# A macaron block with mixture-of-experts layers: indirect transfers of two kinds without an upper bound for their indices

## The reference

```python
x = x + 0.5 * ffn(layernorm(x))      # mixture of experts
x = x + attn(layernorm(x))           # gate, long convolution, gated projections
x = x + 0.5 * ffn(layernorm(x))      # the same mixture again

def ffn(x):                          # E = 12 experts, K = 3 for each token, hidden size 512
    gate_logits = x @ Wg
    topw, sel = top_k(gate_logits, 3); topw = softmax(topw)
    h = gelu(x @ Wup[e] + bup[e])    # for each expert e that the token chose
    y = h @ Wdown[e] + bdown[e]
    return sum over the 3 experts of topw * y
```

## Time and profile before

| | |
|---|---|
| median of 3 runs | 943.9 us (943.35 to 944.24) |
| span of the profiled execution, first to last instruction | 623.9 us |
| outside the span | 320.0 us by the median |
| PE busy | 560.0 us |
| ACT busy | 514.5 us |
| GpSimd (POOL) busy | 416.4 us |
| DVE busy | 373.2 us |

### The profile page before, as it was taken

How to read it: one execution, slowest core, us unless ns; L and a number is a source line. 1 busy time by engine, 2 the same in 40 slices (tenths; PEclk the granted TensorE clock), 3 DMA queues, 4 the chain that set the end, 5 groups by cost and what they waited for, 6 DMA issues and landing times.

```text
span 623.9 us, 17393 instructions
## 1 busy us (share of the span) xinstructions
PE 560.0 (90%) x4527; PEld 522.7 (84%) x4527; DVE 373.2 (60%) x1735; ACT 514.5 (82%) x1462; POOL 416.4 (67%) x424
## 2 busy tenths in 40 slices
PE   7559879999999999999899799998798799999995
PEld 6449779999999888878889688787698799999992
DVE  7947788653111577888865679987828532232224
ACT  3557777599998989899889699998589679998984
POOL 1074557677776777327677777777777777777770
PEclk9999988899999999999999799999799989999997
DMA  7996242343454343312255333332264532433264
GB/s 192 323 222 190 63 113 67 86 123 87 128 161 128 104 119 101 80 45 67 72 169 133 90 87 98 90 98 70 69 153 109 131 87 70 117 87 83 61 225 136
DMA packets 99127, 72.28 MB, mean 116 GB/s; under 512 B 13520, under 2 KB 91910, under 8 KB 99033
## 3 DMA queue, kind: packets, MB, share of 16 engines
q1 hardware_dynamic: 83032, 43.62, 25.5%
q0 software_dynamic: 13024, 26.11, 14.9%
q10 hardware_dynamic: 2976, 1.44, 0.9%
HBM read 37.08 MB, written 34.75 MB: 115 GB/s over the span
## 4 chain that ended last, share of the span: by engine, by line
PE 38%; DVE 15%; POOL 14%; issue 11%; DMA 11%; ACT 6%; SPq 3%; ACTq 1%; DVEq 1%; POOLq 0%
PE ps L1001 16%; PE ps L1014 15%; POOL YG L807 11%; DMA yk<-Ys,row 4%; DMA YG<-ys,SY 3%; ACT hT L1184 2%; POOL yk L818 2%; DVE YG L1698 2%; SPq L607 1%; PE ps L971 1%; DVE X L1311 1%; DVE st L1255 1%; DVE Ys L2037 1%; PE ps L961 1%; DMA xl<-xna,SG 1%
## 5 line engine op out<-in xcount | busy, mean ns | idle before, releaser
L1184 ACT ACTIVATE hT<-ps,BU 128x128 f32<-128x128 f32 x900 | 260.5, 390 | 52.8 <-PE ps L1001 42.0
L1014 PE MATMUL ps<-WD,hT 128*128 x1800 | 245.0, 281 | 18.8 <-DVE Ys L2037 18.7
L1001 PE MATMUL ps<-xT,WT 128*128 128x128 f32 x1800 | 248.7, 283 | 5.9 <-ACT xT L1174 3.0
L1014 PEld LDWEIGHTS ps<-WD,hT 128*128 128x128 f32 x1800 | 224.6, 196 | 22.2 <-issue 22.1
L1001 PEld LDWEIGHTS ps<-xT,WT 128*128 128x128 f32 x1800 | 228.5, 198 | 15.3 <-issue 11.7
L790 POOL DMA_INDIRECT xs<-XN,SX x144 | 146.6, 1018 | 64.6 <-issue 58.1
L807 POOL DMA_INDIRECT YG<-ys,SY x132 | 135.6, 1027 | 43.3 <-issue 35.3
L2037 DVE TENSOR_TENSOR Ys<-ps,BD 128x128 f32<-128x128 f32 x225 | 63.9, 288 | 165.9 <-PE ps L1014 158.5
L1067 ACT ACTIVATE WT<-WU 128x512 f32 x225 | 149.9, 667 | 7.0 <-DVE eW L1731 3.5
L818 POOL DMA_INDIRECT yk<-Ys,row x71 | 70.9, 999 | 21.7 <-issue 12.5
L777 POOL DMA_INDIRECT xl<-xna,SG x24 | 24.3, 1013 | 40.9 <-DMA xna<-XN 27.4
(11 more groups left out here) (366 smaller groups left out, 583.8 us busy)
## 6 DMA issues: line engine op xcount, KB each, us to landing
ys<-Ys SPq DMA_DIRECT2D x41, 256.0 KB
xl<-xs SPq DMA_DIRECT2D x94, 64.0 KB
xl<-xs SPq DMA_DIRECT2D x71, 66.0 KB
WU<-in_L_ffn_Wup_dram SPq DMA_DIRECT2D x12, 256.0 KB, 5.0
WD<-in_L_ffn_Wdown_dram SPq DMA_DIRECT2D x12, 256.0 KB, 5.2
YG<-yk SPq DMA_DIRECT2D x4, 768.0 KB, 7.6
xs<-XN,SX POOLq DMA_INDIRECT x144
YG<-ys,SY POOLq DMA_INDIRECT x132
```

The costliest lines, as they stand in the source:

```text
L1001: x = e.matmul(HB[i % 2][:, c * P:(c + 1) * P], WT[i % NW][:, c, :], xT[m % 2][:, j * P:(j + 1) * P], start=True, stop=True)
L1014: x = e.matmul(YB[i % 2][:, 0:D], hT[i % 3][:, c * P:(c + 1) * P], WDf[:, bass.ds(r + c * P, P)], start=(c == 0), stop=(c == C - 1))
L1184: x = e.activation(hT[i % 3][:, c * P:(c + 1) * P], HB[i % 2][:, c * P:(c + 1) * P], ACT.Gelu, bias=BU[:, bass.ds(b + c, 1)])
```

## The change

The scatters of normalised rows (`scatter_x`) and the gathers of results (`gather_y`) are issued without `bounds_check` and without `oob_is_err=False`. `gather_x` and `scatter_y` keep theirs. With them four registers go that held the bounds. No transfer is added, removed or moved, on any queue.

```diff
-            a_top, x_top, row_top, k_top = (e.to_reg(n) for n in (ZERO, T, E * CAP - 1, K * NT[3] * P - 1))
-            y_top = [e.to_reg(n - 1) for n in YROWS]
+            a_top, x_top, k_top = (e.to_reg(n) for n in (ZERO, T, K * NT[3] * P - 1))
...
                 e.indirect_dma_start(
-                    xs[n], bass.IndirectOffsetOnAxis(SX[n][:, k, t:t + 1], 0), XN[:, AT[n] + t, 0:DX[n]], None,
-                    bounds_check=row_top, oob_is_err=False).then_inc(s_air[j % AIR], 16)
+                    xs[n], bass.IndirectOffsetOnAxis(SX[n][:, k, t:t + 1], 0), XN[:, AT[n] + t, 0:DX[n]], None
+                    ).then_inc(s_air[j % AIR], 16)
...
                 e.indirect_dma_start(
                     YG[:, (AT[n] + t) % 16, k, :], None, ys[n],
-                    bass.IndirectOffsetOnAxis(SY[n][:, t // 4, k, t % 4:t % 4 + 1], 0),
-                    bounds_check=y_top[n], oob_is_err=False).then_inc(s_air[j % AIR], 16)
+                    bass.IndirectOffsetOnAxis(SY[n][:, t // 4, k, t % 4:t % 4 + 1], 0)
+                    ).then_inc(s_air[j % AIR], 16)
```

## The result

| | before | after |
|---|---|---|
| median | 941.99 us (20 runs, 933.72 to 950.25) | 948.01 us (20 runs, 942.42 to 955.15) |
| ratio after / before | | 1.0073, 95% interval 1.0054 to 1.0091 |
| span of the profiled execution | 623.9 us | 946.6 us |
| mean granted clock of PE in it | 0.970 | 0.809 |

The forecast was 938.7 us, with a range of 934.0 to 944.6 us. The time is above the range, and the sign is wrong.

The account below looks back on a forecast made before the run. PE looked like the limit by share, with GpSimd's transfers delaying it at places and at the end. Gains of 1.3 + 2.4 + 0.85 + 0.6 = 5.15 us took 943.9 to 938.7 us; range 934.0 to 944.6 us.

Parts of the forecast that it names:

- Its last real wait: GpSimd's wait for rows that ScalarE normalises; after it, to 608.62 us, GpSimd was said never to wait beyond its usual gap.
- four terms of the sum: Gains: PE stalls around 345 us 1.3, approach to the last stage 2.4, stall at 559.84 us 0.85, end 0.6 us.
- d: Time that one of the 276 changed transfers on GpSimd saves by having no index bound; estimated at 0.05 us.
- The rival on the slow side: In the last stage, 23 alternations of unbounded gathers and bounded scatters cost 0.10 us each: 2.3 us, 946.2 us; chance 0.17.
- Nothing is saved: GpSimd runs the same steps with or without a bound, saving below 0.012 us per transfer: 943.9 us; chance 0.29.
- the cap: The bound is a large part of GpSimd's instruction, 0.15 us or more; PE then limits: about 935.4 us; chance 0.12.
- VectorE's waits near 343 and 498 us: VectorE's waits for gathered results, 3.42 and 4.67 us, forecast to shrink by about 1.2 and 3.7 us.
- PE's stall near 500 us: PE's stall of 1.99 us before 500.45 us, behind a VectorE wait for gathered results; forecast to be gone.

## Why the prediction was wrong

- **The step that failed** is in the first paragraph: "320.0 us lie outside the span ... I leave them as they are and make the sum inside the span." A span of 623.9 us beside a time of 943.9 us says that the profiled execution isn't one of those that were timed. In an ordinary one 1.7 us lie outside. The prediction names this at its end as what no row excludes, but gives it no chance and no price. All its rows were of an execution that none of the timed ones resembles: the fastest of before on record took 932.55 us.
- **"Its last real wait is the one of 1.99 us before 310.14 us"**, and with it the rule that whatever is saved behind it moves everything later. In the ordinary execution GpSimd waits 78.83, 13.44, 16.06, 9.51, 7.84 and 59.59 us, one after the other, before its transfers between 418.59 and 648.17 us. What it saves there it waits. All four terms of the sum (1.3, 2.4, 0.85 and 0.6 us) stand on GpSimd being behind, and none of them came. Where GpSimd was made the bound, with two memsets, the same kind of sum came out right: 6.2 us worked out and 5.7 us measured.
- **The size of d.** Taken as 0.05 us for both kinds; it is 0.053 us for a gather and 0.013 us for a scatter. The range of -0.02 to 0.20 us held both. GpSimd's busy time fell by 411.5 - 402.9 = 8.6 us between ordinary executions, where 14 us were forecast.
- **The Trainium skill's branch price** (GPSIMD Engine Reference, section 3.1), by which a bound would have cost an estimated 1.28 us a transfer, was set aside on the rows. Rightly: 0.053 us for 128 rows is 0.4 ns a row.
- **The rival on the slow side** came out in sign and had the wrong mechanism, and its own price, 946.2 us with a chance of 0.17, lay outside the stated range. Alternation of the two forms costs nothing that shows: line 818's scatters, which have unbounded gathers among them now, have a median of 987 ns after and of 990 ns before. No rival was about what the transfers do to the other engines, and that decided. "Nothing is saved" and the cap are out by d.
- **What was to show it.** The means fell and line 818's stayed, as said. Of VectorE's waits near 343 and 498 us and PE's stall near 500 us nothing can be said: the waits of the ordinary trace are of another kind and size, such as VectorE's 34.01 us before 341.10 us.

What stays open: through what the transfers hold the others up. PE, DVE, ACT and the queue of plain transfers stand still together, at times for 20 us and more, with nothing in the profile that holds them, and the DMA engines are at a share of 0.2 to 0.3. Slower data transfers don't explain it: by the pages, the packets of GpSimd's own DMA queue kept the 16 engines busy for 14.9% of 623.9 = 93 us in the execution without the hold-up and for 9.5% of 946.6 = 90 us in after, those of the largest plain queue for 25.5% and 16.6%, 159 and 157 us. It also stays open what was different in the execution of 623.9 us, in which gathers 1.33 us apart in the mean let PE go on. So close spacing alone is not enough for the hold-up; some condition that this execution lacked belongs to it. It was not seen again in any profile of the study.

The Trainium skill, Perfetto Trace Analysis, section "Identifying the Most-Contended Engine", says to optimise first the engine that is busy for the largest share. Here that is PE (67%, and 61% by its weight loads), and GpSimd at 43% is the last but one. The runs disagree: 18.5% came from letting GpSimd work less densely, with no work taken off PE.

## What to carry to other kernels

Compare the span with the timed median before anything else; here they differed by 320 us, the trace was of another kind of execution than the times, and no sum made on its waits held. Where several engines stand still together with no visible holder, look at what the remaining engine does at that time, and try to space it out: a shorter instruction on it can cost more than it saves. Dropping the index bound of an indirect transfer took 0.05 us off a gather of 128 rows and 0.01 us off a scatter, and this helped only where GpSimd was the bound.

## What the runs showed of the hardware

- Indirect transfers that GpSimd issues 1.25 to 1.30 us apart, for 20 us and more, nearly stopped the other engines in every ordinary execution that was profiled: 0 to 16 matrix products in the stretches of 20 us from 300 or 310 us, against 181 with GpSimd idle. At 1.43 us apart there were 40, at 1.92 us 137, and in the last stage of after, at 1.6 us, 150. One execution of before, at 1.33 us, was free of it.
- The stall is not tied to GpSimd's busy time. In the kernel with one memset it is busy for 16.2 us of 20 and PE runs 40 products; with two it is busy for 13.8 us; in before for 15.4 us with 16 products.
- A memset that is waited for put the gathers 0.13 us further apart when it was the only one (1.304 to 1.431 us), and a second 0.52 us more (to 1.948 us): the idle time before the next transfer goes from 0.27 to 0.56 us.
- PE's granted clock stands at 0.50 in the held-up stretches from 300 to 330 us, after up to 21 us without a product; that is the lower of its two levels (1.2 GHz). It is at 1.00 where PE works on, with GpSimd idle (250 to 270 us of after) or with two memsets between its transfers. Part of the lost time is this: PE is busy for 634.3 us instead of 560.0 us, and 8 products took 2.07 us in the held-up stretch of after, and 1.15 us at 345.63 us in the earlier trace rows.
